# A decoder layer on one core: four moves in the order of the first pipeline turns

## The chip, the cores and the metric

One core of a Trainium2 chip runs the kernel. The metric is the time of one execution on the device in microseconds (us), lower is better. Five engines work side by side, each through its own list of instructions: TensorE (PE, its weight loads PEld), VectorE (DVE), ScalarE (ACT), GpSimd (POOL) and SyncE (SP), which here only issues transfers. They wait for each other by semaphores.

## The reference

One decoder layer over 16 blocks of 128 tokens, 256 channels, in float32. Three residual steps follow each other:

```python
x = x + attn(layernorm(x), Wq, Wk, Wv, Wo, head_scales)     # 8 heads, 2 key/value heads, causal; for each head a
                                                            # mix of softmax attention and a "geometric" attention
x = x + wkv(time_decay, time_first, layernorm(x), ctx)      # k = layernorm(x), v = ctx: a running sum along the
                                                            # tokens, e^k and e^k*v with a decay for each channel
x = x + ffn(layernorm(x), w_gate, w_up, w_down)             # Hadamard rotation, 8-bit activations, ternary weights
```

The head mix is linear in the two attentions, so the kernel folds `1 - head_scales` and `head_scales` into the rows of `Wo` once, at the start. The running sum uses a table of decays and two small guard values for each channel, also made once.

## The kernel before

The first phase does the attention and the running sum for 16 blocks, the second the feed-forward part. The change is in the first phase, which takes roughly the first 285 us.

The first phase is a pipeline written out by hand. Each engine has a function `body` which it calls once a turn, and each turn works on several blocks at different stages. For TensorE, ScalarE and GpSimd, turn r has: stage f, block r (projection, rotation, splitting); stage m, block r-1 (scores, row maxima, exponentials); stage b, block r-2 (attention output, `Wo`, first residual, statistics of the second layernorm); stage c, block r-3 (exponentials of the running sum and their products with the context); stage d, block r-4 (the sums' quotient, second residual). VectorE has one stage more, e, one block ahead of f: it normalizes the block that f takes next. So VectorE's `e[0] == 2` is reached in turn 1 of the others and `e[0] == 3` in turn 2. A turn is counted here by TensorE, from its first mask matmul for the scores (L459).

What sets the order of the work is the order of the code alone: each engine goes through its list and stops at a wait, and all that is behind stands still with it. Names used below:

- `a_xn` (L762): normalized input of block e; TensorE turns it (L476) early in the next turn. It needs `mv` and `rstd`; `statistics(g)` (L618) makes them for four blocks at a time on VectorE up to `a_ve` (L627), and GpSimd's `deviation(g)` (L281) then makes `a_rstd`.
- `a_att` (L779): attention output on VectorE; TensorE's `Wo` product (L586) waits for it, the first residual (L790) for the product, and then come the statistics of the second layernorm (L802 to L812, ending in `b_ve`) and GpSimd's `b_rstd` (L327).
- `b_xn` (L655): normalized input of the running sum. VectorE does it in stage c behind the row maxima `a_mx` (L649); TensorE turns it (L523).
- `b_ev_in`, `b_ev_now` (L318, L322): GpSimd's products with the context block `vT[p]`, ahead of `b_rstd` in the same turn.
- `guard`, `guard_n`, `first_g`, `decay` (L747 to L757): the tables of the running sum; ScalarE's first exponentials of stage c wait for them.
- `w_o` (L638 to L644): the scaled output weights, from `w_o_raw` and `hs_in`.

On SyncE, all loads of the start are issued in one row. At its end stand:

```python
sp.dma_start(had256[:, :, :], ...)           # used in the second phase
sp.wait_ge(s_wabs, 3)                        # ScalarE has read had_f's room for the third time
sp.dma_start(had_f[:, :], t["h512"])         # 1 MB
...
load(0, 0)                                   # context blocks 0 and 1 into vT
load(1, 1)
```

`had_f` shares its room with `w_junk`, into which ScalarE writes the absolute values of the three feed-forward weights in turns 1, 2 and 3 (L440, which counts `s_wabs`).

Of the kernel before, what the change touches and what calls it, by code (L numbers as in the profile page):

```python
# [10 lines left out]
ALU = mybir.AluOpType  # L11
# [3 lines left out]
P = 128  # L15
NB = 16
C = 256
KC = C // P
H, KVH, DH = 8, 2, 32
# [13 lines left out]
T1 = P + 1  # L33
# [38 lines left out]
def decoder_layer(nc, t, out):  # L72
    with ExitStack() as ctx:
# [74 lines left out]
        with ExitStack() as ph:  # L148
# [83 lines left out]
            def _(sp):  # L232
# [22 lines left out]
                sp.dma_start(had256[:, :, :], t["h256"].rearrange("(k p) n -> p k n", p=P)).then_inc(s_ffc, 16)  # L255
                sp.wait_ge(s_wabs, 3)
                sp.dma_start(had_f[:, :], t["h512"]).then_inc(s_ffc, 16)
                cv = t["ctxT"].rearrange("(k c) b t -> c k b t", k=KC)
# [7 lines left out]
                load(0, 0)  # L266
                load(1, 1)
                with sp.Fori(1, NB // 2) as j:
                    load(2 * j, 0)
                    load(2 * j + 1, 1)  # L270
# [7 lines left out]
            def _(pool):  # L278
# [10 lines left out]
                def body(f, m, b, c, d):  # L289
# [7 lines left out]
                    if f is not None:  # L297
                        u, p = f
                        need(pool, A["hi"], 2 * (u + 1))
                        need(pool, A["tq"], u - 1)  # L300
                        qv = split_q[p][:, :].rearrange("t (h s d) -> t h s d", h=H, s=2)
                        nc.gpsimd.tensor_tensor(  # L302
                            qv[:, :, 1, :], qk[p][:, 0:H * DH].rearrange("t (h d) -> t h d", h=H),
                            qv[:, :, 0, :].bitcast(F32), ALU.subtract).then_inc(A["lo"], 1)
                        kv = split_k[p][:, :].rearrange("t (s g r d) -> t s g r d", s=2, g=KVH, r=4)
                        nc.gpsimd.tensor_tensor(
                            kv[:, 1], spread(qk[p][:, H * DH:QKW].rearrange("t (g d) -> t g d", g=KVH), 2, 4),
                            kv[:, 0].bitcast(F32), ALU.subtract).then_inc(A["lo"], 1)
                        if isinstance(u, int) and u < 3:
                            deviation(u + 1)  # L310

                    if c is not None:
                        u, p = c
                        need(pool, s_vT[p], 16 * (u // 2 + 1) if isinstance(u, int) else 8 * (u - p) + 16)
# [17 lines left out]
            def _(act):  # L332
# [14 lines left out]
                def body(f, m, b, c, d):  # L347
# [17 lines left out]
                    if f is not None:  # L365
                        u, p = f
                        need(act, A["rot"], 3 * (u + 1))
                        if isinstance(u, int) and u == 4:
                            act.wait_ge(s_wq, 1)
                        need(act, A["vn"], u - 1)  # L370
                        nc.scalar.copy(v_in[p][:, :], pj[:, QKW:PW]).then_inc(A["v"], 1)
                    if c is not None:
                        u, p = c

                        if isinstance(u, int) and u == 0:
                            act.wait_ge(s_grd, 4 + KC)
# [46 lines left out]
                    if f is not None:  # L423
# [3 lines left out]
                        nc.scalar.copy(qkT[p][:, :], scores[:, :]).then_inc(A["qT"], 1)  # L427
                        if isinstance(u, int) and u == 2:

# [4 lines left out]

                        if isinstance(u, int) and 1 <= u <= 3:
# [6 lines left out]
                    if m is not None and (not isinstance(m[0], int) or m[0] >= 4):  # L442
                        ternary(m[0] - 4)
# [4 lines left out]
            def _(pe):  # L448
# [3 lines left out]
                def body(f, m, b, c, d):  # L452
# [47 lines left out]
                    if f is not None:  # L500
                        u, p = f
                        if isinstance(u, int) and u == 0:
# [4 lines left out]
                        if isinstance(u, int) and u == 4:  # L507

# [24 lines left out]
                    if b is not None:  # L533
# [5 lines left out]
                        if f is not None:  # L539
                            need(pe, A["v"], f[0] + 1)  # L540
                            if isinstance(u, int) and u == 2:
                                pe.wait_ge(s_wq, 1)
# [24 lines left out]
                    if f is not None:  # L567
                        u, p = f
                        if isinstance(u, int) and u == 0:
                            pe.wait_ge(s_cst, 3)  # L570
# [8 lines left out]
                    if b is not None:  # L579
                        u, p = b  # L580
                        if isinstance(u, int) and u == 0:
                            pe.wait_ge(s_wox, REP)
# [19 lines left out]
            def _(dve):  # L602
# [31 lines left out]
                def body(e, f, m, b, c, d):  # L634
                    if e is not None and isinstance(e[0], int) and e[0] == 2:

                        dve.wait_ge(s_wold, 4 * KVH * 16)
                        nc.vector.tensor_scalar(head_mix[0:64, :], hs_in[0:64, :], -1.0, 1.0, ALU.mult, ALU.add).then_inc(s_mix, 1)  # L638
                        nc.vector.tensor_copy(head_mix[64:P, :], hs_in[64:P, :]).then_inc(s_mix, 1)
                        dve.wait_ge(s_mix, 2)  # L640

                        for i, h in enumerate((0, 2, 1, 3)):
                            nc.vector.tensor_scalar(w_o[:, i, :], w_o_raw[:, h, :], head_mix[:, h:h + 1], None,
                                                    ALU.mult).then_inc(s_wox, 1)  # L644
                    if m is not None:
# [33 lines left out]
                    if f is not None:  # L679
# [9 lines left out]
                        if isinstance(u, int) and u == 4:  # L689

# [28 lines left out]
                    if f is not None:  # L719
# [13 lines left out]
                        nc.vector.tensor_reduce(proj_d[p][:, :], dv, AX.X, ALU.add).then_inc(A["dir"], 1)  # L733
                    if e is not None and isinstance(e[0], int) and e[0] == 5:
                        dve.wait_ge(s_wq, 1)
# [3 lines left out]
                        nc.vector.tensor_copy(w_inv[:, :].rearrange("p (n k) -> p n k", n=3), every).then_inc(s_wq, 1)  # L739
                    if e is not None and isinstance(e[0], int) and e[0] < 4:  # L740
                        if e[0]:
                            statistics(e[0])
                        if e[0] == 3:
                            dve.wait_ge(A["rstd"], 4)
                            dve.wait_ge(s_dld, 2 * 16)

                            nc.vector.tensor_scalar(guard[:, :], first_in[:, :], 0.0, None, ALU.max).then_inc(s_grd, 1)  # L747
                            nc.vector.memset(decay[:, :], 0.0).then_inc(s_grd, 1)
                            dve.wait_ge(s_grd, 2)
                            nc.vector.tensor_scalar(guard_n[:, :], guard[:, :], -1.0, None, ALU.mult).then_inc(s_grd, 1)  # L750
                            nc.vector.tensor_tensor(first_g[:, :], first_in[:, :], guard[:, :], ALU.subtract).then_inc(s_grd, 1)

                            dve.wait_ge(s_dcy, 2)
                            for k in range(KC):
                                nc.vector.tensor_scalar(decay[:, k * T1 + 1:(k + 1) * T1],
                                                        ones[:, :],
                                                        decay_e[:, k:k + 1], None, ALU.mult).then_inc(s_grd, 1)  # L757
# [6 lines left out]
                    if e is not None and isinstance(e[0], int) and e[0] == 0:  # L764
                        dve.wait_ge(s_idn, 16)
# [20 lines left out]
                    if b is not None:  # L786
                        u, p = b
                        need(dve, A["wo"], u + 1)
                        need(dve, B["yt"], u - 1)
                        nc.vector.tensor_tensor(x_res[:, u, :], x_res[:, u, :], wo_o, ALU.add).then_inc(A["x1"], 1)  # L790
                    if d is not None:
                        u, p = d
# [497 lines left out]
```

## Time and profile before

| what | value |
|---|---|
| time, median of 3 runs | 484.73 us (483.17 to 489.6) |
| the profiled execution | 479.27 us |
| its span in the trace | 477.4 us |
| busy: PE, DVE, ACT, POOL | 393.3, 330.7, 258.3, 152.4 us |

The profiled execution has a time of its own, 1.87 us above its span. It lies 5.5 us below the median of the three timed runs. Sums are made against the profiled execution and then carried to the median. A mean clock of 1.00 in a row is TensorE at 2.4 GHz, 0.50 at 1.2 GHz.

### The profile page before, as it was taken

How to read it: one execution, taken by the hardware profiler on the slowest of the kernel's cores; microseconds unless marked ns; L12 is line 12 of the kernel's file. 1: busy time of each engine (PE TensorE's matmuls, PEld its weight loads, DVE VectorE, ACT ScalarE, POOL GpSimd, SP SyncE). 2: the span in 40 equal slices, each digit the busy share in tenths (PEclk: the TensorE clock that was granted, in tenths of full speed). 3: DMA queues.
4: the chain of work that ended last, by engine and by line, in shares of the span. 5: the costliest groups of instructions: out<-in, count | busy, mean ns of one | idle time of the engine just before them, and what ended most of it. 6: DMA issues, size and time to landing. Idle time of an engine off the chain costs nothing. (4 is left out here: it accounts for less than half of the span.)

```text
span 477.4 us, 7507 instructions
## 1 busy us (share of the span) xinstructions
PE 393.3 (82%) x2306; PEld 256.7 (54%) x2306; DVE 330.7 (69%) x865; ACT 258.3 (54%) x482; POOL 152.4 (32%) x161
## 2 busy tenths in 40 slices
PE   2578795999999999999998732579899989999795
PEld 1345353445655545655555211357677767777573
DVE  3563573697777797677867663368888898897642
ACT  1124553556577766577646432354685675856542
POOL 1230231443445443354514030134333333332310
PEclk9666799699999999899989885568999999999899
DMA  8920003000000000000000000000000000000000
GB/s 247 295 80 1 0 2 121 13 0 13 11 14 12 0 13 12 12 12 12 1 12 12 11 1 2 0 0 0 2 12 12 15 9 23 12 13 23 11 24 33
DMA packets 13642, 13.14 MB, mean 28 GB/s; under 512 B 2004, under 2 KB 12884, under 8 KB 13476
## 3 DMA queue, kind: packets, MB, share of 16 engines
q1 hardware_dynamic: 13604, 12.67, 8.8%
q8 instruction: 19, 0.31, 0.3%
q14 instruction: 19, 0.16, 0.1%
HBM read 10.57 MB, written 2.10 MB: 27 GB/s over the span
## 5 line engine op out<-in xcount | busy, mean ns | idle before, releaser
L884 POOL TENSOR_TENSOR c_h_lo<-c_hb,c_h_hi 128x512 fp32r<-128x512 f32 x32 | 40.7, 1270 | 72.8 <-ACT c_h_hi L927 67.5
L1022 PE MATMUL wide<-had,c_h_hi 128*128 128x512 f32 x128 | 54.2, 423 | 7.5 <-ACT c_q2T L938 7.5
L1022 PE MATMUL wide<-had,c_h_lo 128*128 128x512 f32 x128 | 51.4, 401 | 0.0
L1008 PE MATMUL wide<-c_q_T,w_tern_all 128*128 128x256 bf16 x256 | 39.5, 298 | 8.2 <-DVE c_hh L1120 6.8
L790 DVE TENSOR_TENSOR x_res<-x_res,bank 128x256 f32<-128x256 f32 x16 | 6.7, 421 | 48.3 <-PE bank L597 41.8
L586 PE MATMUL bank<-w_o,a_att 128*128 128x256 f32 x128 | 36.1, 432 | 4.6 <-issue 3.3
L296 POOL TENSOR_TENSOR a_qk<-a_rot_c,a_rot_s 128x320 f32<-128x320 f32 x16 | 15.4, 961 | 76.1 <-DVE a_rot_s L687 76.1
L302 POOL TENSOR_TENSOR a_split_q<-a_qk,a_split_q 128x256 fp32r<-128x256 f32 x16 | 34.1, 2134 | 15.3 <-ACT a_split_k L394 15.3
L921 ACT ACTIVATE c_sl<-c_z 128x512 f32<-128x512 f32 x32 | 20.1, 628 | 30.5 <-DVE c_z L1111 30.4
L563 PE MATMUL wide<-a_g_diag,a_row_sb 40*128 40x512 f32 x64 | 33.9, 652 | 2.6 <-DVE a_g_diag L706 2.6
L1008 PEld LDWEIGHTS wide<-c_q_T,w_tern_all 128*128 128x128 bf16 x256 | 24.7, 105 | 21.2 <-DVE c_hh L1120 9.3
L1022 PEld LDWEIGHTS wide<-had,c_h_hi 128*128 128x128 f32 x128 | 24.6, 192 | 14.0 <-issue 9.3
L586 PEld LDWEIGHTS bank<-w_o,a_att 128*128 128x128 f32 x128 | 25.8, 211 | 9.9 <-issue 4.2
L327 POOL TENSOR_TENSOR b_rstd<-b_ve,neg_half 128x1 f32<-128x1 f32 x16 | 8.8, 550 | 68.1 <-DVE b_ve L812 68.1
L1111 DVE SCALAR_TENSOR_TENSOR c_z<-wide,w_scale,c_s_row 128x512 f32<-128x512 f32 x32 | 23.8, 743 | 8.7 <-PE wide L1008 7.8
L1133 DVE TENSOR_REDUCE c_am<-wide 128x1 f32<-128x1024 f32 x16 | 19.5, 1218 | 13.3 <-PE wide L1022 13.3
L1120 DVE TENSOR_TENSOR c_hh<-wide,c_sl 128x512 f32<-128x512 f32 x32 | 22.1, 691 | 9.2 <-ACT c_sl L921 9.2
L352 ACT COPY a_xT<-bank 128x256 f32<-128x256 f32 x16 | 6.0, 372 | 39.2 <-PE bank L476 39.2
L1022 PEld LDWEIGHTS wide<-had,c_h_lo 128*128 128x128 f32 x128 | 24.7, 193 | 4.5
L514 PE MATMUL bank<-w_qkv,a_xT 128*128 128x384 f32 x64 | 25.7, 527 | 0.6 <-ACT a_xT L352 0.6
L649 DVE TENSOR_REDUCE a_mx<-wide 128x8 f32<-128x1024 f32 x16 | 19.6, 1224 | 7.0 <-PE wide L467 6.9
L422 ACT ACTIVATE a_e_g<-wide 128x1024 f32<-128x1024 f32 x16 | 16.4, 1027 | 14.0 <-PE wide L563 14.0
(168 smaller groups left out, 1016.7 us busy)
## 6 DMA issues: line engine op xcount, KB each, us to landing
x_res<-in_x SPq DMA_DIRECT2D x4, 512.0 KB, 7.5
b_vT<-in_ctxT SPq DMA_DIRECT2D x16, 128.0 KB, 2.2
out<-c_yo SPq DMA_DIRECT2D x16, 128.0 KB, 1.7
w_raw_all<-in_wg SPq DMA_DIRECT2D x1, 1024.0 KB, 9.1
w_raw_all<-in_wu SPq DMA_DIRECT2D x1, 1024.0 KB, 11.4
w_raw_all<-in_wd SPq DMA_DIRECT2D x1, 1024.0 KB, 13.7
had_f<-in_h SPq DMA_DIRECT2D x1, 1024.0 KB, 5.0
w_o_raw<-in_Wo SPq DMA_DIRECT2D x4, 128.0 KB, 6.3
```

The lines of the kernel that those rows point to most:

```text
L302: nc.gpsimd.tensor_tensor(qv[:, :, 1, :], qk[p][:, 0:H * DH].rearrange("t (h d) -> t h d", h=H), qv[:, :, 0, :].bitcast(F32), ALU.subtract ...
L514: mm = nc.tensor.matmul(pj[:, 0:PW], xT[p][:, k * P:k * P + P], w_qkv[:, k, :], start=(k == 0), stop=(k == KC - 1))
L563: mm = nc.tensor.matmul(geo[:, g * 512:g * 512 + 512], k_row[p][:, :], g_diag[p][:, g * 512:g * 512 + 512], start=False, stop=True, skip_g ...
L586: mm = nc.tensor.matmul(wo_o, att[p][:, i * P:i * P + P], w_o[:, i, :], start=(i == 0), stop=(i == REP - 1))
L649: nc.vector.tensor_reduce(mx[p][:, :], scores[:, :].rearrange("t (h s) -> t h s", h=H), AX.X, ALU.max).then_inc(A["mx"], 1)
L884: nc.gpsimd.tensor_tensor(h_lo[p][:, j::FQ, :], hb[j % 2][:, :].rearrange("c (m t) -> c m t", m=2), h_hi[p][:, j::FQ, :].bitcast(F32), ALU ...
L921: nc.scalar.activation(sl[j % 2][:, :], z[j % 2][:, :], ACT.Silu).then_inc(D["sl"], 1)
L1008: mm = nc.tensor.matmul(dst[:, m * TOK:(m + 1) * TOK], w[:, k * FF + blk * P:k * FF + blk * P + P], q_T[p][:, k * TOK:(k + 1) * TOK], star ...
L1022: mm = nc.tensor.matmul(wide[:, 1 + i, m * 512:(m + 1) * 512], a[p][:, j + FQ * m, i * P:(i + 1) * P], had512[:, j, :], start=(j == 0 and ...
L1111: nc.vector.scalar_tensor_tensor(out=two_(z[j % 2][:, :]), in0=two_(gate), scalar=w_scale[:, 0:1], in1=spread(s_row[p][:, :], 1, 2), op0=A ...
L1120: nc.vector.tensor_tensor(hh[j % 2][:, :], up, sl[j % 2][:, :], ALU.mult).then_inc(D["h"], 1)
L1133: nc.vector.tensor_reduce(am2[p][:, c], wide[:, 1 + i, :], AX.X, ALU.max, apply_absolute_value=True).then_inc(D["am2"], 1)
```

## The change

Four moves, and tests of a kind of number that are left out since the pipeline is wholly written out (`isinstance(u, int)`, no instruction changes):

1. SyncE issues the loads of context blocks 0 and 1 behind the feed-forward weights, ahead of `had256` and of the wait for `s_wabs`.
2. VectorE makes the guard and decay tables behind the first residual of block 0, not ahead of `a_xn` of block 3 and `a_att` of block 0.
3. The one wait for all four `a_rstd` ahead of the tables goes; `a_xn` of blocks 0, 4, 8 and 12 waits for the one of its group.
4. VectorE scales the output weights behind `a_proj_d` (L733), not at the start of its turn ahead of `a_mx`.

```diff
+                load(0, 0)
+                load(1, 1)
                 sp.dma_start(had256[:, :, :], t["h256"].rearrange("(k p) n -> p k n", p=P)).then_inc(s_ffc, 16)
                 sp.wait_ge(s_wabs, 3)
                 sp.dma_start(had_f[:, :], t["h512"]).then_inc(s_ffc, 16)
...
-                load(0, 0)
-                load(1, 1)
...
-                        if e[0] == 3:
-                            dve.wait_ge(A["rstd"], 4)
-                            dve.wait_ge(s_dld, 2 * 16)
...
                     if e is not None:
                         u, p = e
                         need(dve, A["t1"], u - 1)
+                        if u % 4 == 0:
+                            dve.wait_ge(A["rstd"], u // 4 + 1)
```

SyncE, the end of its row of first loads, before and after (`had` is `had256`, `had_f` the 1 MB one):

```order
 L253 DMA w_raw_all<-in_wu 128x2x1024
 L253 DMA w_raw_all<-in_wd 128x8x256
-L255 DMA had<-in_h 128x2x256
-L257 DMA had_f<-in_h 128x2048
-L264 DMA b_vT<-in_ctxT 128x2x128 x2
+L261 DMA b_vT<-in_ctxT 128x2x128 x2
+L265 DMA had<-in_h 128x2x256
+L267 DMA had_f<-in_h 128x2048
```

The two context loads stand ahead of both Hadamard matrices and of the wait between these.

VectorE in turn 2, before: from the last group's deviations' input to the statistics of block 0 after its first residual.

```order
L627 TENSOR_SCALAR a_ve<-a_mv 128x4
L747 TENSOR_SCALAR guard<-first_in 128x2
L748 MEMSET decay 128x258
L750 TENSOR_SCALAR guard_n<-guard 128x2
L751 TENSOR_TENSOR first_g<-first_in,guard 128x2
L755 TENSOR_SCALAR decay<-ones,decay_e 128x128 x2
L762 TENSOR_SCALAR a_xn<-x_res,a_mv,a_rstd 128x256
L779 TENSOR_TENSOR a_att<-bank,a_inv 128x512
L790 TENSOR_TENSOR x_res<-x_res,bank 128x256
L802 MEMSET b_carry 128x1
```

The same place on VectorE after (line numbers shift, the instructions are the same):

```order
L627 TENSOR_SCALAR a_ve<-a_mv 128x4
L748 TENSOR_SCALAR a_xn<-x_res,a_mv,a_rstd 128x256
L765 TENSOR_TENSOR a_att<-bank,a_inv 128x512
L776 TENSOR_TENSOR x_res<-x_res,bank 128x256
L780 TENSOR_SCALAR guard<-first_in 128x2
L781 MEMSET decay 128x258
L783 TENSOR_SCALAR guard_n<-guard 128x2
L784 TENSOR_TENSOR first_g<-first_in,guard 128x2
L788 TENSOR_SCALAR decay<-ones,decay_e 128x128 x2
L802 MEMSET b_carry 128x1
```

The tables stand now behind the residual add of block 0 and ahead of its second statistics.

VectorE at the end of turn 1, after: where the output weights are scaled now.

```order
L723 TENSOR_REDUCE a_proj_d<-a_dq 128x16
L727 TENSOR_SCALAR head_mix<-hs_in 64x4
L728 COPY head_mix<-hs_in 64x4
L732 TENSOR_SCALAR w_o<-w_o_raw,head_mix 128x256 x4
L622 BN_STATS a_st<-x_res 128x6 x4
```

Before, these three rows stood at the start of the turn, ahead of `a_mx`.

## Rows read from the trace of the kernel before

**Rows 1.** Busy time by turn (2, 3, 4, 5): us, each engine, PEclk, DMA.

```profile
37.38:58.66 21.28, 17.55 (x83) 10.17 (x84) 10.59 (x31) 10.21 (x18) 4.38 (x4) 0.74 0.00 1
58.66:72.89 14.23, 13.86 (x86) 8.12 (x85) 9.35 (x23) 7.57 (x17) 3.83 (x4) 0.93 0.01 2
72.89:95.63 22.74, 17.24 (x90) 9.18 (x89) 11.62 (x31) 9.37 (x20) 7.63 (x8) 0.77 0.21 70
95.63:109.89 14.26, 13.27 (x89) 7.81 (x87) 11.11 (x29) 8.76 (x20) 6.24 (x6) 1.00 0.00 0
```

**Rows 2.** Waits, first 130 us: total us, times, longest.

```profile
POOL b_ev_in L318 <- DMA b_vT<-in_ctxT: 10.1, 1, 10.1
...
DVE b_xn L655 <- POOL b_rstd L327: 6.0, 1, 6.0
...
PE wide L523 <- DVE b_xn L655: 4.3, 1, 4.3
```

**Rows 3.** Timeline, turn 2 into 3: start, us, instruction, idle before.

```profile
51.32 0.50 PE L576 MATMUL wide<-ident_r,a_split_k 128*128 128x128 f32 x4
51.70 0.17 DVE L627 TENSOR_SCALAR a_ve<-a_mv 128x4 f32<-128x4 f32 x1
...
53.00 0.17 DVE L747 TENSOR_SCALAR guard<-first_in 128x2 f32<-128x2 f32 x1 [1.13 <-POOL a_rstd L283]
...
54.01 0.41 DVE L762 TENSOR_SCALAR a_xn<-x_res,a_mv,a_rstd 128x256 f32<-128x256 f32 x1
54.34 0.68 DVE L779 TENSOR_TENSOR a_att<-bank,a_inv 128x512 f32<-128x512 f32 x1
...
55.12 3.75 PE L586 MATMUL bank<-w_o,a_att 128*128 128x256 f32 x8 [3.29 <-issue]
...
61.31 1.22 DVE L649 TENSOR_REDUCE a_mx<-wide 128x8 f32<-128x1024 f32 x1 [1.04 <-PE wide L467]
```

**Rows 4.** Timeline, end of turn 3 and turn 4.

```profile
69.81 0.68 DVE L779 TENSOR_TENSOR a_att<-bank,a_inv 128x512 f32<-128x512 f32 x1
...
71.10 1.96 PE L586 MATMUL bank<-w_o,a_att 128*128 128x256 f32 x8
...
73.10 0.42 DVE L790 TENSOR_TENSOR x_res<-x_res,bank 128x256 f32<-128x256 f32 x1 [2.60 <-PE bank L586]
...
74.31 0.16 DVE L812 TENSOR_TENSOR b_ve<-b_mv,b_ve 128x1 f32<-128x1 f32 x1
74.35 0.34 SPq L257 DMA_DIRECT2D had_f<-in_h  x1
...
74.57 1.22 DVE L649 TENSOR_REDUCE a_mx<-wide 128x8 f32<-128x1024 f32 x1
...
81.79 0.41 DVE L655 TENSOR_SCALAR b_xn<-x_res,b_mv,b_rstd 128x256 f32<-128x256 f32 x1 [5.99 <-POOL b_rstd L327]
```

**Rows 5.** Timeline, turn 1 into 2: output weights and their neighbours.

```profile
21.28 1.14 DVE L643 TENSOR_SCALAR w_o<-w_o_raw,head_mix 128x256 f32<-128x256 f32 x4
...
22.34 1.22 DVE L649 TENSOR_REDUCE a_mx<-wide 128x8 f32<-128x1024 f32 x1
...
24.52 0.37 PE L496 MATMUL wide<-ident,a_mx 128*8 128x128 f32 x1
...
33.97 0.17 DVE L627 TENSOR_SCALAR a_ve<-a_mv 128x4 f32<-128x4 f32 x1
34.05 0.41 DVE L762 TENSOR_SCALAR a_xn<-x_res,a_mv,a_rstd 128x256 f32<-128x256 f32 x1
...
40.24 0.69 PE L476 MATMUL bank<-ident,a_xn 128*128 128x128 f32 x2
```

**Rows 6.** Groups by line, 96 to 290 us: count, busy us, mean ns, idle before.

```profile
L779 DVE TENSOR_TENSOR a_att<-bank,a_inv 128x512 f32<-128x512 f32 x13 | 8.8, 679 | 0.9 <-PE bank L552 0.6 <-ACT a_inv L409 0.3
...
L762 DVE TENSOR_SCALAR a_xn<-x_res,a_mv,a_rstd 128x256 f32<-128x256 f32 x10 | 5.9, 595 | 0.0
```

**Rows 7.** Busy time of a later turn in which the clock fell, columns as in Rows 1.

```profile
181.25:197.11 15.86, 14.93 (x90) 8.85 (x87) 11.11 (x29) 10.08 (x21) 6.23 (x6) 0.90 0.06 18
```

More of the change, by code:

```diff
@@ L267, in _ @@
                 load(1, 1)
+                sp.dma_start(had256[:, :, :], t["h256"].rearrange("(k p) n -> p k n", p=P)).then_inc(s_ffc, 16)
+                sp.wait_ge(s_wabs, 3)
+                sp.dma_start(had_f[:, :], t["h512"]).then_inc(s_ffc, 16)
                 with sp.Fori(1, NB // 2) as j:
@@ L367, in body @@
                         need(act, A["rot"], 3 * (u + 1))
[L368 removed]
+                        if u == 4:
                             act.wait_ge(s_wq, 1)
@@ L373, in body @@
                         u, p = c
-                        if isinstance(u, int) and u == 0:
+                        if u == 0:
                             act.wait_ge(s_grd, 4 + KC)
@@ L441, in body @@
                                                  accum_out=w_abs[:, n:n + 1]).then_inc(s_wabs, 1)
-                    if m is not None and (not isinstance(m[0], int) or m[0] >= 4):
+                    if m is not None and m[0] >= 4:
                         ternary(m[0] - 4)
@@ L501, in body @@
                         u, p = f
-                        if isinstance(u, int) and u == 0:
+                        if u == 0:
                             pe.wait_ge(s_wld, 3 * 16)
@@ L506, in body @@
                         need(pe, B["x2"], u - 4)
-                        if isinstance(u, int) and u == 4:
+                        if u == 4:
                             need(pe, A["rot"], 3 * u)
@@ L568, in body @@
                         u, p = f
-                        if isinstance(u, int) and u == 0:
+                        if u == 0:
                             pe.wait_ge(s_cst, 3)
@@ L580, in body @@
                         u, p = b
-                        if isinstance(u, int) and u == 0:
+                        if u == 0:
                             pe.wait_ge(s_wox, REP)
@@ L733, in body @@
                         nc.vector.tensor_reduce(proj_d[p][:, :], dv, AX.X, ALU.add).then_inc(A["dir"], 1)
-                    if e is not None and isinstance(e[0], int) and e[0] == 5:
+                    if e is not None and e[0] == 2:
+                        dve.wait_ge(s_wold, 4 * KVH * 16)
+                        nc.vector.tensor_scalar(head_mix[0:64, :], hs_in[0:64, :], -1.0, 1.0, ALU.mult, ALU.add).then_inc(s_mix, 1)
+                        nc.vector.tensor_copy(head_mix[64:P, :], hs_in[64:P, :]).then_inc(s_mix, 1)
+                        dve.wait_ge(s_mix, 2)
+                        for i, h in enumerate((0, 2, 1, 3)):
+                            nc.vector.tensor_scalar(w_o[:, i, :], w_o_raw[:, h, :], head_mix[:, h:h + 1], None,
+                                                    ALU.mult).then_inc(s_wox, 1)
+                    if e is not None and e[0] == 5:
                         dve.wait_ge(s_wq, 1)
@@ L739, in body @@
                         nc.vector.tensor_copy(w_inv[:, :].rearrange("p (n k) -> p n k", n=3), every).then_inc(s_wq, 1)
-                    if e is not None and isinstance(e[0], int) and e[0] < 4:
+                    if e is not None and e[0] < 4:
                         if e[0]:
                             statistics(e[0])
-                        if e[0] == 3:
-                            dve.wait_ge(A["rstd"], 4)
-                            dve.wait_ge(s_dld, 2 * 16)
[L747 to L757, printed above, removed]
                     if e is not None:
@@ L790, in body @@
                         nc.vector.tensor_tensor(x_res[:, u, :], x_res[:, u, :], wo_o, ALU.add).then_inc(A["x1"], 1)
+                    if e is not None and e[0] == 3:
+                        dve.wait_ge(s_dld, 2 * 16)
+                        nc.vector.tensor_scalar(guard[:, :], first_in[:, :], 0.0, None, ALU.max).then_inc(s_grd, 1)
+                        nc.vector.memset(decay[:, :], 0.0).then_inc(s_grd, 1)
+                        dve.wait_ge(s_grd, 2)
+                        nc.vector.tensor_scalar(guard_n[:, :], guard[:, :], -1.0, None, ALU.mult).then_inc(s_grd, 1)
+                        nc.vector.tensor_tensor(first_g[:, :], first_in[:, :], guard[:, :], ALU.subtract).then_inc(s_grd, 1)
+                        dve.wait_ge(s_dcy, 2)
+                        for k in range(KC):
+                            nc.vector.tensor_scalar(decay[:, k * T1 + 1:(k + 1) * T1],
+                                                    ones[:, :],
+                                                    decay_e[:, k:k + 1], None, ALU.mult).then_inc(s_grd, 1)
                     if d is not None:
```

25 lines of the change are left out of this document (7 added, 18 removed).

## Prediction

> **What bounds the kernel now.** The change touches only the first turns of the first phase, so I read that stretch and leave the rest aside. First the busy time by turn: turns 3 and 5 take 14.23 and 14.26 us, turn 2 takes 21.28 and turn 4 takes 22.74, with TensorE's mean granted clock at 0.74 and 0.77 in the two long ones against 1.00 in turn 5 [rows 1]. TensorE is what the good turns are full of (13.27 of 14.26 us busy); the long turns hold stalls, and part of their work runs at 1.2 GHz after these. Then the waits of the stretch, to see who stands for whom. The longest single wait with a transfer at its end is GpSimd's, 10.1 us for the first context block; behind it `b_xn` on VectorE waits 6.0 us for GpSimd's `b_rstd`, and TensorE 4.3 us for `b_xn` [rows 2]. That is one chain: the load stands on SyncE behind `had_f`, which is issued only at 74.35 [rows 4] when ScalarE has read the third weight; `b_rstd` of block 1 has nothing to do with the context, but it stands behind the two products on GpSimd. Last the timeline of turn 2: TensorE ends its transposes at 51.82 and starts the `Wo` product at 55.12, an idle time of 3.3 us [rows 3]. The view names "issue" as the releaser, but the program shows that the product needs `a_att`, and that ended at 55.02. `a_att` came late because VectorE first waited 1.13 us for GpSimd's last `a_rstd` and then made the tables.
>
> **Part 1, the tables behind the residual (turn 2).** Before, `a_ve` starts at 51.70, the tables at 53.00, `a_xn` at 54.01, `a_att` at 54.34, the product at 55.12 [rows 3]. Now `a_xn` follows `a_ve` directly; the two stand 0.08 us apart in start where nothing is between them (33.97 and 34.05 [rows 5]), so it starts at 51.78. `a_att` follows 0.33 us later (54.34 - 54.01), at 52.11, and the product 0.78 us behind that (55.12 - 54.34), at 52.89: 2.23 us earlier. TensorE then idles 52.89 - 51.82 = 1.07 us instead of 3.3.
>
> What the product costs depends on the clock. Before, it took 3.75 us at the low clock [rows 3]; one turn later, without an idle time ahead, 1.96 us [rows 4]. I take 1.96. Then the residual of block 0 starts 2.00 us after the product (73.10 - 71.10), at 54.89. From the residual to the end of `b_ve` it is 74.31 + 0.16 - 73.10 = 1.37 us [rows 4], and the tables now lie in between with 54.01 - 53.00 = 1.01 us [rows 3] (all their inputs are there by then): `b_ve` ends at 57.27, and `a_mx` of block 2 can start 0.10 us later (74.57 - 74.47), at 57.37. Without the tables it would start 74.57 - 71.10 = 3.47 us after the product, as it does one turn later [rows 4], at 56.36. So the tables are not free in this case: they are what is late next, on VectorE, and take back 1.0 us. Before, `a_mx` started at 61.31 [rows 3]. Part 1 is worth 61.31 - 57.37 = **3.94 us**. If the clock is low for the product all the same, everything moves by 2.23 us only, and then the tables are covered: `a_mx` had 1.04 us of idle time ahead of it [rows 3], against their 1.01. So the ends of this term are 2.2 and 3.9. The Trainium skill, page "TensorE: Matmul & The Clock Gate", Part 1, says that what the gate goes by runs free of the kernel's start, so that one kernel changes clock at different points from run to run. By that rule both ends would occur among executions of the same kernel; the trace, a single execution, can't show it.
>
> **Part 2, the context loads (turn 4).** Two loads of 128 KB move ahead of `had256`, which the first phase never reads, and ahead of a wait that ends at 74.35. They are issued right behind the weights of the start, and GpSimd asks for them only at the end of turn 3. GpSimd's products of block 0 then run directly behind its splits at the end of turn 3, and `b_rstd` of block 1 follows `b_ve` (74.47), so `b_xn` starts when `a_mx` ends, at 74.57 + 1.22 = 75.79 instead of 81.79 [rows 4]: 6.0 us. The rest of the loss is the low clock behind the stall: 22.74 - 14.26 = 8.48 us is what turn 4 has more than turn 5 [rows 1], 2.5 us of it beyond those 6.0. With no stall I expect turn 4 to be as turn 5 is. It has four small VectorE or TensorE instructions that turn 5 has not (the sums of the weights and their scale), each of the size of `a_ve` (0.17 us [rows 3]), which make 0.7 us if nothing hides them. I charge 0.1, since VectorE's lie ahead of `a_att`, which has 0.61 us of cover (below). So 22.74 - 14.26 - 0.1 = **8.4 us**, between 7.8 and 8.5. The loads of blocks 2 and 3 stay behind `had_f`, which also comes 3.9 us earlier, and are not needed before turn 5.
>
> The early products are new neighbours for VectorE at the end of turn 3, where `a_xn` and `a_att` run. In the later turns GpSimd works beside these two: there `a_att` takes 0.679 us in the mean, as in turns 2 and 3 where it took 0.68, and `a_xn` 0.595 against 0.41 alone [rows 3, 5, 6]. So I charge nothing; between `a_att`'s end and the product there are 71.10 - 70.49 = 0.61 us of cover [rows 4]. If `a_att` had to stand off for both products (taken at `a_att`'s own length, 1.4 us), 0.8 us of it would show; that is the upper bound, and the later turns lie far from it.
>
> **Part 3, the split waits.** The single wait for all deviations cost 1.13 us and is counted in part 1. The new ones, for blocks 4, 8 and 12, ask for values that are there a turn or more before: nothing, at most one smallest VectorE step each.
>
> **Part 4, the output weights.** They take 1.14 us and 0.4 us of preparation on VectorE, ahead of `a_mx` [rows 5]. `a_mx` ended at 23.56 and TensorE came to it at 24.52, busy until then, so taking them away from there gives nothing. In their new place they push `a_xn` of block 2 from 34.05 to some 35.6, and TensorE reads it at 40.24 [rows 5]: covered with 4.2 us to spare. GpSimd's `a_rstd` of the third group moves with it, and is read eight blocks on. Zero.
>
> **The sum.** 3.94 + 8.4 = 12.3 us. The profiled execution took 479.27 us, so it would be 467.0. The timed median lies higher, at 484.73, and its three runs span 6.4 us; carried over, 484.73 - 12.3 = 472.4. Nothing behind turn 4 gives it back: the later turns have a period of their own, and the second phase starts when the first ends.
>
> **The rivals.** First, the clock falls in turn 2 after all. For: it has fallen later in this trace without any idle time, in the turn from 181.25 to 197.11, which lasted 15.86 us at a mean clock of 0.90 [rows 7]; in turn 2 the same weak stretch (the 40-row products and transposes) is followed by 1.07 us of idleness. Against: 1.07 is a third of what it was. Then part 1 is 2.2: 484.73 - 10.6 = 474.1.
>
> Second, turn 4 finds another late partner and stays slow. VectorE is nearly as loaded there as TensorE (11.62 us of work in that turn [rows 1]), and if the clock falls in it too, only the plain idle times go: 2.23 + 4.3 = 6.5 us, 478.2. Against it stands turn 5, which has the same work and needs 14.26.
>
> Third, slower than before: the clock falls in many of the later turns instead of a few. Place: the stretch of each turn just ahead of the `Wo` product. Price: 15.86 - 14.26 = 1.6 us for each turn [rows 1, 7]. The 11 turns behind turn 4 held two such falls; if shifting them made it all 11, that is 9 x 1.6 = 14.4 us lost against 12.3 won: 486.8. It decides from 8 further falls on. Nothing but chance would put them all there.
>
> Fourth, the change frees more than the sum: a turn 3 in which the tables too are hidden, and fewer falls (the two of before gone, 3.2 us): 484.73 - 12.3 - 1.0 - 3.2 = 468.2.
>
> **How the numbers follow.** Forecast 472.4, chance 0.47. Clock falls in turn 2: 0.30. Turn 4 stays slow: 0.12. Slower: 0.02. More: 0.09. Two per cent, about what a measurement of this kernel can tell from no change, is 9.7 us, so the line lies at 475.0. The forecast reaches it by 2.6 us and the first rival by 0.9, each with one or two falls of the clock of 1.6 us as its scatter: of the forecast I count nine tenths as faster, of the first rival six tenths, of the last all. That is 0.42 + 0.18 + 0.09 = 0.69; slower by over 2% 0.01; the rest 0.30. The range goes from just below the fourth rival to just above the second, 467.5 to 478.5: it holds nearly all of the forecast and of the first rival and some half of the other two, and leaves out less than 2 in 10.
>
> **What would show it.** In the trace after: turn 4 near 14.3 us with a clock of 1.00, no wait of `b_ev_in` for its load, `b_xn` of block 1 directly behind `a_mx`; an idle time of about 1.1 us ahead of the first `Wo` product, which takes 1.96 us (or about 3.7, the first rival); `a_mx` of block 2 directly behind `b_ve`; the same `a_att`. I am wrong if turn 4 is above 16 us, if the gap ahead of the first product stays above 2 us, or if the gain comes in part from turns that the change doesn't touch.

## The result and the profile after

The changed kernel takes **466.25 us** (median of four runs, 464.53 to 472.41), the kernel before 484.36 (483.17 to 489.6): ratio 0.9594 [0.9503, 0.9686], with its 95 per cent interval. Medians here are taken over all runs, ratios with their intervals over those within 1.5% of the fastest of their kernel. The median is 18.1 us lower; 12.3 were forecast, and it lies 1.25 us below the low end of the range. Two later comparisons of the same two kernels gave 11.6 and 13.1 us less; their intervals are clear of 1 but reach above 0.98. Over all 16 runs of the changed kernel the median is 468.77 (464.53 to 474.66), over 55 of the kernel before 482.69 (475.22 to 489.6): 13.9 us. With 8 more runs of the kernel before, described below, it is 482.01, and the difference 13.2. So there are two questions: do the two repaired turns account for some 14 us, and why did one comparison give 18.

The busy time of the kernel after by turns 1 to 5 (stretch and length, then busy us and instructions of TensorE, its weight loads, VectorE, ScalarE and GpSimd, granted clock, DMA share, GB/s), to be compared with [rows 1]:

```profile
19.42:35.77 16.35, 12.67 (x58) 7.52 (x60) 10.01 (x28) 5.23 (x11) 3.35 (x3) 0.71 0.51 173
35.77:53.87 18.10, 16.37 (x83) 9.36 (x85) 10.11 (x29) 9.70 (x17) 5.58 (x5) 0.78 0.00 1
53.87:67.77 13.90, 12.79 (x86) 7.56 (x85) 10.19 (x29) 8.10 (x19) 5.23 (x6) 1.00 0.01 2
67.77:81.95 14.18, 13.22 (x90) 8.03 (x90) 11.63 (x31) 9.37 (x20) 6.36 (x6) 1.00 0.25 85
81.95:96.20 14.25, 13.16 (x88) 7.80 (x87) 11.11 (x29) 8.76 (x20) 6.24 (x6) 1.00 0.03 9
```

Turn 4 is now as short as turn 5, at full clock, though the later context loads and the 512 Hadamard move 85 GB/s in it. Turn 2 is 3.2 us shorter than in [rows 1], turn 3 0.3. The timeline of the kernel after at the end of turn 2 (start, us, engine and line, operation; in brackets the idle time before it and what ended it), to be compared with [rows 3]:

```profile
50.88 0.17 DVE L627 TENSOR_SCALAR a_ve<-a_mv 128x4 f32<-128x4 f32 x1
50.95 0.41 DVE L748 TENSOR_SCALAR a_xn<-x_res,a_mv,a_rstd 128x256 f32<-128x256 f32 x1
51.28 0.68 DVE L765 TENSOR_TENSOR a_att<-bank,a_inv 128x512 f32<-128x512 f32 x1
52.06 1.97 PE L586 MATMUL bank<-w_o,a_att 128*128 128x256 f32 x8 [1.07 <-issue]
54.07 0.42 DVE L776 TENSOR_TENSOR x_res<-x_res,bank 128x256 f32<-128x256 f32 x1 [2.10 <-PE bank L586]
54.41 0.16 DVE L780 TENSOR_SCALAR guard<-first_in 128x2 f32<-128x2 f32 x1
55.02 0.48 DVE L788 TENSOR_SCALAR decay<-ones,decay_e 128x128 f32<-128x128 f32 x2
56.27 1.22 DVE L639 TENSOR_REDUCE a_mx<-wide 128x8 f32<-128x1024 f32 x1
57.55 0.27 PE L496 MATMUL wide<-ident,a_mx 128*8 128x128 f32 x1 [0.57 <-DVE a_mx L639]
```

The tables (L780 to L788) stand behind the residual, and the first `Wo` product runs after 1.07 us of idle time, the forecast number, in 1.97 us. What is late next is also the instruction that was named: `a_mx`, behind the tables on VectorE, and TensorE waits 0.57 us for it. The same view around the start of turn 4, to be compared with [rows 4]:

```profile
63.85 0.77 POOL L306 TENSOR_TENSOR a_split_k<-a_qk,a_split_k 128x256 fp32r<-128x256 f32 x1
64.58 0.73 POOL L318 TENSOR_TENSOR b_ev_in<-b_e_in,b_vT 128x256 f32<-128x256 f32 x1
...
69.18 0.16 DVE L812 TENSOR_TENSOR b_ve<-b_mv,b_ve 128x1 f32<-128x1 f32 x1
69.23 0.34 SPq L267 DMA_DIRECT2D had_f<-in_h  x1
...
69.42 0.56 POOL L327 TENSOR_TENSOR b_rstd<-b_ve,neg_half 128x1 f32<-128x1 f32 x1 [3.40 <-DVE b_ve L812]
69.45 1.22 DVE L639 TENSOR_REDUCE a_mx<-wide 128x8 f32<-128x1024 f32 x1
70.59 0.40 DVE L645 TENSOR_SCALAR b_xn<-x_res,b_mv,b_rstd 128x256 f32<-128x256 f32 x1
```

`b_ev_in` follows GpSimd's split without a wait for its load, `b_rstd` follows `b_ve`, and `b_xn` starts when `a_mx` ends. The 10.1, 6.0 and 4.3 us of [rows 2] are gone.

Turn by turn, from the same view of several kernels (us; "rest" is from the start of TensorE's last turn to the end of the span, that is the last block's drain and the second phase):

| kernel | turn 1 | turns 2+3 | turn 4 | turns 5 to 15 | rest | span |
|---|---|---|---|---|---|---|
| before | 18.35 | 35.51 | 22.74 | 160.23 | 221.5 | 477.4 |
| before, second profile | 18.36 | 35.52 | 25.86 | 161.88 | 217.5 | 478.2 |
| output weights alone | 18.79 | 35.85 | 25.89 | 161.63 | 221.4 | 482.5 |
| changed | 16.35 | 32.00 | 14.18 | 156.60 | 224.1 | 462.6 |
| changed, second | 16.35 | 31.24 | 14.16 | 160.17 | 225.0 | 466.0 |
| changed, third | 16.34 | 31.40 | 14.17 | 160.25 | 223.2 | 464.4 |
| loads alone | 16.28 | 37.52 | 14.16 | 158.44 | 220.4 | 465.8 |
| tables alone | 18.80 | 31.45 | 21.63 | 160.04 | 224.0 | 475.0 |

Between the means of the first three rows and of the next three: turn 1 -2.2, turns 2 and 3 -4.1, turn 4 -10.7, the later turns -2.2, the rest +4.0, and the start (up to turn 1) +0.2; together -15.0 us of span.

### The profile page after: what moved, and what is told of

Read it like the earlier page. It is cut to its first block and busy times, and to the rows that moved or that the text cites. A ratio compares the mean times of both kernels' runs of the same rounds, so it can differ in the third digit from the quotient of the medians.

```text
span 462.6 us, 7493 instructions
## 1 busy us (share of the span) xinstructions
PE 383.4 (83%) x2290; PEld 252.8 (55%) x2306; DVE 331.9 (72%) x865; ACT 258.3 (56%) x482; POOL 152.0 (33%) x161
## 5 line engine op out<-in xcount | busy, mean ns | idle before, releaser
L1008 PE MATMUL wide<-c_q_T,w_tern_all 128*128 128x256 bf16 x256 | 38.3, 292 | 8.3 <-DVE c_hh L1120 6.9
L586 PE MATMUL bank<-w_o,a_att 128*128 128x256 f32 x128 | 33.3, 405 | 1.9 <-issue 1.1
L563 PE MATMUL wide<-a_g_diag,a_row_sb 40*128 40x512 f32 x64 | 31.7, 615 | 2.6 <-DVE a_g_diag L696 2.6
L586 PEld LDWEIGHTS bank<-w_o,a_att 128*128 128x128 f32 x128 | 24.1, 198 | 7.4 <-DVE a_att L765 2.5
L552 PE MATMUL bank<-a_e_s,ones 128*32 128x512 f32 x64 | 18.5, 654 | 5.4 <-issue 4.2
## 6 DMA issues: line engine op xcount, KB each, us to landing
w_raw_all<-in_wd SPq DMA_DIRECT2D x1, 1024.0 KB, 12.3
```

The lines of the kernel that those rows point to most:

```text
L563: mm = nc.tensor.matmul(geo[:, g * 512:g * 512 + 512], k_row[p][:, :], g_diag[p][:, g * 512:g * 512 + 512], start=False, stop=True, skip_g ...
L586: mm = nc.tensor.matmul(wo_o, att[p][:, i * P:i * P + P], w_o[:, i, :], start=(i == 0), stop=(i == REP - 1))
L1008: mm = nc.tensor.matmul(dst[:, m * TOK:(m + 1) * TOK], w[:, k * FF + blk * P:k * FF + blk * P + P], q_T[p][:, k * TOK:(k + 1) * TOK], star ...
```

## The experiments

The first question was whether the two repaired turns carry the gain, as forecast, or whether one move alone is worth more than its turn (the output weights, for instance, by way of turn 1). Four kernels ran on one chip beside the kernel before (482.86).

**The loads alone**: the kernel before, with only this.

```diff
-sp.dma_start(had256[:, :, :], ...)
-sp.wait_ge(s_wabs, 3)
-sp.dma_start(had_f[:, :], t["h512"])
 ...
 load(0, 0)
 load(1, 1)
+sp.dma_start(had256[:, :, :], ...)
+sp.wait_ge(s_wabs, 3)
+sp.dma_start(had_f[:, :], t["h512"])
```

> Only the two context loads move; tables, waits and output weights stay as before. Theory A (the stalls that were foreseen are the whole direct gain, and the rest of the 18 us between the medians is which executions met which falls of the clock): turn 4 falls from 22.7 to 14.2 us, turn 2 stays at 21.3, the median falls by 8.5 us, give or take 3 for the clock. Theory B (one part is worth more than was foreseen): the same turn 4, but 12 us or more of the 18.

Measured: 468.84 us, 0.9745 [0.9697, 0.9792]. Its busy time by turn (turns 1, 2, 4):

```profile
19.05:35.33 16.28, 12.83 (x60) 7.31 (x60) 10.21 (x29) 5.22 (x11) 4.46 (x4) 0.90 0.52 179
35.33:56.96 21.63, 17.84 (x83) 10.36 (x84) 10.58 (x31) 10.21 (x18) 4.38 (x4) 0.74 0.00 1
...
72.85:87.01 14.16, 13.37 (x90) 8.03 (x89) 11.61 (x31) 9.37 (x20) 6.33 (x6) 1.00 0.25 85
```

Turn 4 is mended and turn 2 is as long as before, at the same clock of 0.74. (Turn 3 took 15.89 here, at a fall of the clock.) The median, though, is 14.0 us lower than the kernel before, which is theory B's mark and not theory A's: turn 4 gives 8.6 to 11.7 of it, and turn 1 was 2.1 us shorter in this profile.

**The tables alone** (with the split waits): the changed kernel with loads and output weights back in their old places.

> Only the tables move behind the first residual, with the split waits for the deviations; loads and output weights as before. Theory A: turn 2 and 3 together 3.5 us shorter (2.2 if the clock is low for the first Wo product), turn 4 stays at 22.7, median 3.5 us lower, give or take 3. Theory B: 6 us or more.

Measured: 476.22 us, 0.9848 [0.979, 0.9906]. Turns 2 and 4 in the same view:

```profile
37.94:55.48 17.54, 15.96 (x83) 9.10 (x84) 9.52 (x25) 9.70 (x17) 4.47 (x4) 0.81 0.00 1
...
69.39:91.02 21.63, 16.10 (x90) 8.88 (x89) 11.56 (x31) 9.38 (x20) 7.64 (x8) 0.84 0.21 74
```

Turn 2 is mended and turn 4 is long. In the traces each move mends its own turn and leaves the stall in the other's. The median is 6.6 us lower, just outside theory A's range and past theory B's mark: turns 2 and 3 give 4.1 us, and turn 4, with its stall still there, ran at a clock of 0.84 and took 21.63 us, 1.1 less than in the first profile before.

**The output weights alone**: the kernel before with the block that scales `w_o` moved behind `a_proj_d`.

> Only the scaling of the output weights moves. Theory A: nothing, within 2 us of the kernel before, turn 1 between 16.3 and 18.4 us by the clock at its 40-row products alone. Theory B: the 2 us that turn 1 lost in the profile of the whole change (18.35 to 16.35) come from this move, so the median is 2 us or more lower and turn 1 is near 16.3.

Measured: 483.49 us, 1.0009 [0.9966, 1.0053], and turn 1 took 18.79. Part 4 is worth nothing, as forecast, and the rival that gave it turn 1's gain falls (turn 1 came out 0.4 us above the expected 16.3 to 18.4).

**The changed kernel again**, unedited, to see what one program does in another profile.

> The changed kernel once more, on the same chip as its parts. Theory A: 12 us below the kernel before, with a scatter of some 3; the sum of the parts within 3 us of it. Theory B: 18 us again, ratio 0.96, while the parts as foreseen add up to 12.

Measured: 471.25 us, 0.9785 [0.9731, 0.984]. Turns 2, 4 and 10:

```profile
35.46:52.80 17.34, 15.82 (x83) 9.08 (x84) 9.52 (x25) 9.70 (x17) 5.25 (x5) 0.82 0.00 1
...
66.70:80.86 14.16, 13.36 (x90) 8.03 (x89) 11.61 (x31) 9.39 (x20) 6.33 (x6) 1.00 0.24 85
...
152.18:168.09 15.91, 14.98 (x89) 8.91 (x87) 11.10 (x29) 10.11 (x21) 6.22 (x6) 0.89 0.06 18
```

The repaired turns repeat to 0.8 and 0.02 us. What differs is behind them: two later turns at a clock of about 0.9 and 1.6 us longer, where the first profile had none. A third profile (in the table) also has two.

By time the parts do not add up: 14.0 + 6.6 - 0.6 = 20.0 us, where the whole gave 11.6 on the same chip, and theory A had them within 3. The loads alone (468.84) even did as well as the whole change (471.25 here, 468.77 over all its runs). In the profiles the changed kernel's turns 2 and 3 are 5.5 to 6.3 us shorter than with the loads alone (1.6 of it the fall in turn 3 there), but its rest is 2.8 to 4.6 us longer. That the other three moves shorten the whole beyond the loads is therefore shown in turns 2 and 3, and not in the time.

> The changed kernel a third time, for a ratio with more runs. Theory A (some 14 us on the average: turn 4 loses 8.6 to 11.7 and turns 2 and 3 some 4): median 12 to 16 us below the kernel before. Rival (the first measurement of 18 us was typical): 17 us or more.

That run gave 468.76 us, 0.9755 [0.9696, 0.9814]. Medians of one program thus lie at 466.25, 471.25 and 468.76.

The second question was what turn 4 had really cost. **The kernel before again**, unedited:

> The kernel before, for a second profile of it. Theory A (turns 2 to 4 hold the gain of 12 us, the rest is the luck of the clock): the same stalls in turns 2 and 4 as in the first profile (21.3 and 22.7 us within 1.5), and a different number of later turns of 15.9 us. Rival (before's timed runs hold a stall that its first profile did not show, of some 5 us): one turn or the second phase some 5 us longer, with the clock at 1.00.

Measured: 481.38 us against 481.73 for the other runs of this kernel beside it. Its turns 2 and 4:

```profile
37.47:58.76 21.29, 17.55 (x84) 10.18 (x85) 10.58 (x31) 10.22 (x18) 4.38 (x4) 0.74 0.00 1
...
72.99:98.85 25.86, 20.47 (x91) 10.90 (x90) 11.61 (x31) 9.48 (x20) 7.63 (x8) 0.67 0.18 62
```

Turn 2 is the same to 0.01 us, turn 4 is 3.1 us longer, twice the 1.5 that theory A allowed, with no turn longer at a clock of 1.00. TensorE's timeline in the second half of that turn, first of the execution that the prediction was read from:

```profile
82.26 0.69 PE L523 MATMUL wide<-ident,b_xn 128*128 128x128 f32 x2 [4.33 <-DVE b_xn L655]
84.13 1.97 PE L529 MATMUL wide<-a_m_row,pick_neg 40*128 40x128 f32 x8 [1.18 <-DVE a_m_row L677]
...
90.56 2.42 PE L563 MATMUL wide<-a_g_diag,a_row_sb 40*128 40x512 f32 x4
...
93.62 1.96 PE L586 MATMUL bank<-w_o,a_att 128*128 128x256 f32 x8
```

and then of the second profile of that kernel:

```profile
82.24 0.69 PE L523 MATMUL wide<-ident,b_xn 128*128 128x128 f32 x2 [4.21 <-DVE b_xn L655]
84.11 1.96 PE L529 MATMUL wide<-a_m_row,pick_neg 40*128 40x128 f32 x8 [1.18 <-DVE a_m_row L677]
...
90.54 3.78 PE L563 MATMUL wide<-a_g_diag,a_row_sb 40*128 40x512 f32 x4
...
95.31 3.48 PE L586 MATMUL bank<-w_o,a_att 128*128 128x256 f32 x8
```

The waits are the same, 4.2 to 4.3 and 1.18 us, and from 82 to 90.5 the two agree within 0.03 us. Then the first gets back to 2.4 GHz in the middle of L563, and the second stays at 1.2 GHz to within half a microsecond of the turn's end. The same products in turn 4 of the changed kernel, which started at 67.77:

```profile
72.96 1.11 PE L529 MATMUL wide<-a_m_row,pick_neg 40*128 40x128 f32 x8
...
74.94 0.62 PE L552 MATMUL bank<-a_e_s,ones 128*32 128x512 f32 x2
```

This splits the loss. From the turn's start to L529 it is 11.24 us in the first profile, 11.12 in the second and 5.19 in the changed kernel: the waiting costs 5.9 to 6.0 us and repeats. From L529 to the turn's end it is 11.50, 14.74 and 8.99: the low clock behind the wait cost 2.5 us the one time and 5.8 the other. (With the output weights alone the two parts cost 5.9 and 5.8, with the tables alone 5.9 and 1.6.)

**The stall filled**: the kernel before, with the late loads left as they are, and 18 extra products on TensorE in block 1's wait for `b_xn`; their result is never read.

```diff
-need(pe, B["xn"], u + 1)
 need(pe, A["eg"], upto(u + 2, NB))
 need(pe, B["en"], KC * u)
+if u == 1:
+    for _ in range(18):
+        nc.tensor.matmul(wide[:, 2, 512:1024], ident_b[:, :], mask_ts[:, :], start=True, stop=True)
+need(pe, B["xn"], u + 1)
```

> The kernel before, with 18 more mask matmuls on TensorE (into a bank half that is free) in the one place of turn 4 where it waits for the normalized input of block 1; the context loads stay late. Theory A (turn 4 loses 6 us of plain waiting and the rest to the low clock that follows): turn 4 near 20.3 us with the clock at 1.00, against 22.7 to 25.9 in the three profiles with late loads and late tables, so 2.5 to 5.5 us less than the kernel before. Rival (the whole 8 to 12 us is waiting, and the clock follows from it without a cost): turn 4 as before, no gain.

Measured: 478.14 us against 481.86, 0.994 [0.9892, 0.9988]. Its turn 4, and TensorE's timeline in it:

```profile
73.78:94.79 21.01, 18.96 (x108) 10.09 (x107) 11.70 (x31) 9.24 (x20) 7.67 (x8) 0.92 0.24 76
```

```profile
78.65 4.05 PE L523 MATMUL wide<-mask_ts,ident_b 128*128 128x512 bf16 x18
...
84.93 1.34 PE L532 MATMUL wide<-a_m_row,pick_neg 40*128 40x128 f32 x8 [1.43 <-DVE a_m_row L680]
86.53 1.07 PE L555 MATMUL bank<-a_e_s,ones 128*32 128x512 f32 x2 [0.26 <-ACT a_v_in L371]
```

`b_xn` is as late as before, so all that can be won here is clock: 0.92 in that turn, against 0.77 and 0.67 with the stall left empty. The turn is 1.7 us shorter than in the first of these profiles, 4.9 shorter than in the second and with the output weights alone, and 0.6 shorter than with the tables alone. What is left is 21.01 - 14.17 = 6.8 us. Up to L532 (L529 before) it is 11.15 us, so 6.0 of this is the waiting; behind it 0.9 us are lost, against the 2.5 and 5.8 above. Not all of the clock came back: with `a_m_row` late TensorE still idles 1.43 us, and behind that the clock was low once more (L555 takes 1.07 us; the same products, L552, take 0.62 in the changed kernel).

The third question was what the change leaves. **The tables ahead of the residual**: the changed kernel with the table block moved from behind the residual to behind `a_att`, into the time in which VectorE waits for the `Wo` product.

> The changed kernel with the tables one place further forward: behind the attention output, ahead of the first residual, where VectorE waits 2.1 us for the Wo product. Prediction's step (the tables delay the row maxima of block 2 by 1.0 us): turn 3 falls from 13.9 to 13.0 us, the row maxima follow TensorE's scores. Rival (the tables were hidden): turn 3 stays at 13.9. The time moves by less than a measurement shows either way.

Measured: 467.29 us, 0.9721 [0.9615, 0.9827]; the profiled execution took 473.18. Its turn 3, then its timeline:

```profile
54.91:68.18 13.27, 12.90 (x87) 7.56 (x86) 9.35 (x23) 8.11 (x19) 5.22 (x6) 1.00 0.01 2
```

```profile
53.58 0.48 DVE L777 TENSOR_SCALAR decay<-ones,decay_e 128x128 f32<-128x128 f32 x2
55.11 0.42 DVE L790 TENSOR_TENSOR x_res<-x_res,bank 128x256 f32<-128x256 f32 x1 [1.05 <-PE bank L586]
...
57.95 0.27 PE L496 MATMUL wide<-ident,a_mx 128*8 128x128 f32 x1
```

The tables end 1.05 us before the residual can start, L496 has no idle time ahead of it, and turn 3 is 13.27 instead of 13.90: the 0.6 us that the tables take back behind the residual, where the prediction had 1.0. The comparison by time is too coarse to show so little.

**Extra products in turns 1 and 2**: the changed kernel with some 30 products like the one above put into TensorE's waits of the first three turns; again nothing reads their result. The comments are added here.

```diff
+def fill(dst, n):
+    for _ in range(n):
+        nc.tensor.matmul(dst, ident_b[:, :], mask_ts[:, :], start=True, stop=True)
 ...
+if u == 0: fill(bank[0][:, :], 8)    # ahead of the first transposes
+if u < 2: fill(bank[0][:, :], 4)     # behind the transposes
+if u == 0: fill(bank[1][:, :], 5)    # ahead of the first Wo product
```

and 8 more, with the two mask products there once again, ahead of block 0's product with `a_g_diag`.

> The changed kernel with 30 more mask matmuls on TensorE (results overwritten or the same) where it stood idle in turns 0 to 2. Theory A (turns 1 and 2 are still 2 to 4 us longer than turn 3 because they run at 1.2 GHz after idle times): the clock is at 1.00 in both, turn 1 falls from 16.35 to some 13 and turn 2 from 17.7 to some 14.3, 5 to 7 us less in all. Rival (turns 1 and 2 are bound by VectorE and ScalarE, or the extra matmuls stand in the way): no gain, up to 3 us slower.

Measured: 459.1 us, 0.9544 [0.9459, 0.963]. Turns 1 and 2:

```profile
18.71:31.57 12.86, 12.30 (x74) 6.60 (x74) 9.74 (x25) 5.11 (x11) 3.36 (x3) 1.00 0.72 248
31.57:46.06 14.49, 14.03 (x88) 7.74 (x89) 10.38 (x31) 9.67 (x17) 5.57 (x5) 1.00 0.00 0
```

Both turns run at a clock of 1.00 and are 3.5 and 2.9 to 3.6 us shorter than in the changed kernel. What turn 2 had beyond 14.5 us in the changed kernel (17.3 to 18.1) was therefore not waiting, which the products only fill, but a part of its work at 1.2 GHz. Of the 9.7 us between this median and the changed kernel's pooled one (over its 16 runs), the two turns account for 6.3 to 7.1.

**Two extra products in each later turn**: the changed kernel with two such products per block ahead of the transposes into `wide`, from block 2 on.

> The changed kernel with two more full mask matmuls in each turn from turn 2 on, between the 40-row products and the transposes (overwritten by these). Theory A (the later turns of 15.9 us come from this weak stretch): no turn of 15.9 us any more, each turn up to 0.4 us longer, runs within 4 us of each other; the median within 3 us of the changed kernel. Rival (the falls have another origin): turns of 15.9 us stay, on top of 0.2 to 0.4 us for each turn, so 3 to 6 us slower.

Measured: 463.8 us, 0.9645 [0.9557, 0.9734]; the profiled execution took 469.41. One of its turns; those behind it are alike:

```profile
94.97:109.62 14.65, 13.72 (x90) 8.01 (x90) 11.11 (x30) 9.42 (x21) 6.23 (x7) 1.00 0.04 11
```

No later turn falls, and each pays 0.4 us for it (14.65 against 14.25). With falls of 1.6 us in two or three turns of eleven, price and gain are alike; that the median is 5 us below the changed kernel's pooled one is more than this explains. The runs also spread over 10.8 us (461.4 to 472.2), where theory A had 4, and the profiled one, without a fall in turns 3 to 15, lay 5.6 us above the median: the falls of the later turns are not all that spreads the runs.

Put together: the extra products of turns 1 and 2 and the tables ahead of the residual,

> The changed kernel with the extra matmuls in the idle times of turns 0 to 2 and with the tables ahead of the first residual. Turn 1 near 12.9, turn 2 near 14.4, turn 3 near 13.2, turn 4 near 14.2 us: 7 us below the changed kernel, 0.6 of it from the tables. Rival (the two moves share their gain): turn 3 at 13.9 again.

gave 459.88 us, 0.9582 [0.9527, 0.9636], no less than without the tables: turn 3 took 13.26, but the clock fell in turn 4 (15.87). With one extra product in each later turn as well,

> The same with one more mask matmul in each turn from turn 2 on, ahead of the transposes. If half of the dose of two is enough: no turn of 15.9 us, turns of 14.3 to 14.45, and 2 us less than without it. If not: one to three turns of 15.9 us as before, and 0 to 2 us more.

457.34 us, 0.953 [0.947, 0.959], the lowest median, some 11 us below the changed kernel's pooled one. Its turns 2 to 5:

```profile
31.61:46.11 14.50, 14.03 (x89) 7.82 (x90) 11.44 (x37) 9.68 (x17) 5.59 (x5) 1.00 0.00 0
46.11:59.52 13.41, 13.04 (x87) 7.63 (x86) 9.36 (x23) 8.31 (x19) 5.22 (x6) 1.00 0.01 2
59.52:73.86 14.34, 13.54 (x92) 8.12 (x90) 11.61 (x31) 9.26 (x20) 6.34 (x6) 1.00 0.25 85
73.86:88.30 14.44, 13.49 (x91) 7.90 (x88) 11.12 (x29) 8.78 (x20) 6.24 (x6) 1.00 0.03 9
```

Every turn up to the drain stands at 1.00. The intervals of the last two and of the kernel with products in turns 1 and 2 alone overlap, so their order is not settled. Kernels with a product in every later turn were profiled once each, and the changed kernel's first profile had no fall in its later turns either; the other eleven profiles without such a product had one to four.

## Why the prediction was right, and where it was not

**Part 1** held. The idle time ahead of the first `Wo` product is 1.07 us as worked out, the product takes 1.97 (1.96 forecast), and the tables come late next in front of `a_mx`; that they take back 1.0 us was too much, it is 0.6. Turns 2 and 3 together lost 4.1 us in the mean of three profiles each; 3.94 was the term. The first rival, a clock that falls in turn 2, gave no separate outcome: the clock is low in part of that turn in all profiles without extra products in it (0.74 to 0.82), but in the three of the changed kernel it is back for the product, which takes 1.97 us in each.

**Part 2 was mis-sized**, and this is the step that failed: "22.74 - 14.26 = 8.48 us is what turn 4 has more than turn 5", and with it the bounds 7.8 and 8.5. The mechanism was right to the instruction, turn 4 came to 14.18 and not above. But 22.74 was one execution, in which the clock came back early. That was luck: the second execution of the same program stood at the same waits. With late loads and late tables the same turn took 22.74, 25.86 and 25.89, so the repair is worth 8.6 to 11.7 us, 10.7 in the mean (from the 21.63 with the tables alone, one profile, it would be 7.5). The "6.0 us" for the waiting held: 5.9 to 6.0 in each. What was taken as fixed is "2.5 us of it beyond those 6.0", the low clock behind the stall: it measured 2.5, 5.8 and 5.8, and 1.6 with the tables alone, depending on when the clock returned to 2.4 GHz. The bounds covered the cost of the neighbours and left out the one term that varied. The Trainium skill, page "TensorE: Matmul & The Clock Gate", Part 1, says that the gate's reckoning does not start with the kernel; it was quoted for Part 1 of the change, where both ends were allowed. The two traces of the kernel before fit it, with the same waits and another time of return, and they do so in turn 4, for which the prediction didn't draw the consequence. The same page, section "HAM oscillation — how this bites in real kernels", says that behind a long wait for data the next work starts at the low clock. L529 shows that here, with 1.96 to 1.97 us behind the stall and 1.11 in the changed kernel.

**Part 4** cost and gave nothing: the output weights alone came to 1.0009. Part 3 was run only together with part 1, in whose term the prediction counted its gain.

**The second failing step is the carry-over to a median**, and it weighs more: "the timed median lies higher ... carried over", with one or two falls of the clock as its scatter. Terms that the change doesn't aim at moved by more than that. Turn 1 took 16.35 in the three profiles of the changed kernel and 18.35 to 18.8 with late loads; in the kernels with the tables ahead of the residual and with two extra products it was 18.3 again, though both have the early loads. So whether the loads bear on turn 1 stays open. In the later turns none to four falls occurred. Between the means of three profiles turn 1 and the later turns gave 4.4 us, so the prediction's own sign of being wrong, a gain that comes in part from turns that the change doesn't touch, was met. And "nothing behind turn 4 gives it back" did not hold in these profiles: the last block's drain was longer. TensorE's timeline shows how, in the changed kernel:

```profile
261.28 3.78 PE L586 MATMUL bank<-w_o,a_att 128*128 128x256 f32 x8 [0.81 <-DVE a_att L765]
```

and with the loads alone:

```profile
265.49 1.99 PE L586 MATMUL bank<-w_o,a_att 128*128 128x256 f32 x8 [1.30 <-DVE a_att L779]
```

The last product was at 1.2 GHz in the one and at 2.4 in the other. From the start of the last turn to the second phase's first product it was 42.5, 41.8 and 41.7 us in the changed kernel and 39.3 and 38.3 in the kernel before; but 38.3 with early loads alone, and 42.0 and 43.0 in two kernels with late loads and late tables (the output weights alone, the stall filled). That the change causes it is therefore not shown.

**The sums.** The touched turns give 4.1 + 10.7 = 14.8 us against the 12.3 forecast. Turn 1 and the later turns add 4.4, and the rest and the start take 4.1 back. The pooled medians, those over all runs, differ by 13.2 to 13.9. The first comparison's 18.1 is 13.9 plus the chance of two medians: the one after lay 2.5 us below the pooled one, the one before 1.7 above. So of the 5.8 us between 18.1 and 12.3, some 2.3 are turn 4's clock and 4.2 that chance; the other terms nearly cancel. The changed kernel's pooled 468.77 lies inside the range.

Of the rivals, turn 4 did not stay slow and the later turns did not all fall. The fourth had 468.2, close to 468.77, but not for its reasons: it counted a hidden table block, which only the kernel with the tables ahead of the residual has, and no falls in the later turns, which only the first of the three profiles shows.

## What to carry to other kernels

Before a stall is priced from a trace, split it into the wait and the low clock behind it: the wait repeated here (5.9 to 6.0 us), the low clock did not (1.6 to 5.8 us), so the term needs two ends even where every instruction is known. A range for a median has to hold the scatter of medians of one unchanged program, here 5 us, besides the uncertainty of the sum. And add up the times of the parts as well as their turns: here the turns agreed and the times did not, by 8.4 us. Where TensorE must still wait, products whose result nobody reads can pay: in the first turns they went with 9.7 us less. But filling the long stall gave 3.7 us where removing it gave 14.0, so try them once the long waits are gone.

## What the runs showed of the hardware

One product of 128x512 in bf16 per turn, 0.2 us long, went with 11 later turns of 14.38 to 14.44 us at a clock of 1.00, in the one profile of that kernel; without such products 0 to 4 of them took 15.8 to 15.95. No idle time of TensorE announced a fall: in the kernel before, each of these turns, fallen or not, held 0.8 to 1.0 us of idle time (gaps over 0.1 us), in pieces of at most 0.5. The low clock is a sizeable part of this kernel: as the clock counts as 1.00 or 0.50, a mean of 0.900 over 477.4 us in the kernel before means 2 x 0.100 x 477.4 = 95 us at 1.2 GHz; it is 75 in the changed kernel (0.919 of 462.6) and 52 in the last one (0.943 of 454.9). These are times at the low clock, not losses: 43 us fewer of them went with 22.5 us less span, in part from waits that are gone.
